# Condition row first, first group of x in four loads, weight table in 2 KB runs (conditioned residual, one core)

## What is computed

```python
W = weights[condition]                       # (64, 128, 128)
x = x + jnp.einsum('bct,bcd->bdt', x, W)     # (64, 128, 2048)
```

## Time and profile before

| | us |
|---|---|
| median of three runs | 320.84 |
| the profiled execution, its own time | 320.35 |
| its span, first to last instruction | 318.6 |
| PE busy in the span | 244.4 |
| VectorE busy | 146.8 |
| GpSimd busy | 19.0 |

### The profile page before, as it was taken

The page is one execution under the profiler, slowest core; times in us unless marked ns, Lnnn a source line. Parts: engine busy times, 40 slices in busy tenths (PEclk is TensorE's granted clock), DMA queues, the critical chain, the costliest instruction groups (busy, mean ns, idle before and its releaser), DMA issues.

```text
span 318.6 us, 1351 instructions
## 1 busy us (share of the span) xinstructions
PE 244.4 (77%) x512; PEld 103.8 (33%) x512; DVE 146.8 (46%) x65; POOL 19.0 (6%) x69
## 2 busy tenths in 40 slices
PE   0059999996884979969399795948979597596980
PEld 0024444442432424324143342413424242242430
DVE  0005676676261462637326373550745547055371
POOL 0000000000000000000001000000000000001000
PEclk9999999999997897999869799995989999699897
DMA  8999999999999999999999999999999999999997
GB/s 313 436 436 440 416 395 444 411 426 420 440 424 436 444 416 448 424 432 436 428 448 416 444 424 436 444 416 453 416 440 428 432 448 411 453 420 436 440 403 313
DMA packets 5187, 135.29 MB, mean 425 GB/s; under 512 B 578, under 2 KB 578, under 8 KB 578
## 3 DMA queue, kind: packets, MB, share of 16 engines
q10 hardware_dynamic: 2882, 68.16, 49.7%
q1 hardware_dynamic: 2304, 67.11, 49.4%
HBM read 68.16 MB, written 67.11 MB: 425 GB/s over the span
## 4 chain that ended last, share of the span: by engine, by line
DMA 61%; PE 33%; DVE 3%; POOLq 0%; issue 0%; ACTq 0%; POOL 0%
PE product L90 33%; DMA out<-x_ring 29%; DMA x_ring<-x 27%; DMA condition_row<-condition 5%; DVE x_ring L106 3%; POOLq L72 0%; ACTq L111 0%; POOL chosen_weights L78 0%; DVE state_row L100 0%; POOLq L71 0%; POOLq L78 0%; POOLq L77 0%
## 5 line engine op out<-in xcount | busy, mean ns | idle before, releaser
L90 PE MATMUL product<-x_ring,chosen_weights 128*128 128x512 f32 x512 | 244.4, 640 | 64.9 <-DMA x_ring<-x 45.3
L106 DVE TENSOR_TENSOR x_ring<-product,x_ring 128x2048 f32<-128x2048 f32 x64 | 146.7, 2292 | 147.4 <-PE product L90 147.4
L90 PEld LDWEIGHTS product<-x_ring,chosen_weights 128*128 128x128 f32 x512 | 103.8, 205 | 204.6 <-issue 141.1
L78 POOL COPY chosen_weights<-weight_table 128x128 f32 x64 | 18.8, 294 | 286.0 <-DVE x_ring L106 267.2
L100 DVE TENSOR_SCALAR state_row<-condition_row 1x64 int32<-1x64 int32 x1 | 0.2, 182 | 17.3 <-DMA condition_row<-condition 17.3
L137 POOL MEMSET const-float32-0.0<- 128x1 f32 x1 | 0.1, 98 | 0.1
L137 POOL MEMSET const-bfloat16-1.0<- 128x1 bf16 x1 | 0.1, 101 | 0.0
L137 POOL MEMSET const-uint8-127<- 128x1 uint8 x1 | 0.1, 101 | 0.0
L137 POOL MEMSET const-float32-1.0<- 128x1 f32 x1 | 0.1, 98 | 0.0
L137 POOL BASE_LOAD x1 | 0.0, 12 | 0.1
## 6 DMA issues: line engine op xcount, KB each, us to landing
x_ring<-x SPq DMA_DIRECT2D x16, 4096.0 KB, 28.2
out<-x_ring ACTq DMA_DIRECT2D x15, 4096.0 KB, 29.8
out<-x_ring ACTq DMA_DIRECT2D x4, 1024.0 KB, 7.9
weight_table<-weights ACTq DMA_DIRECT2D x1, 1024.0 KB, 15.1
condition_row<-condition ACTq DMA_DIRECT2D x1, 0.2 KB
```

Source lines behind the costliest of these rows:

```text
L78: pool.tensor_copy(chosen_weights[b][:, :], weight_table[:, bass.ds(state[b] * features, features)]).then_inc(weights_chosen[b], 1)
L90: last = pe.matmul(product[:, b % psum_slots, m * BANK_COLUMNS:(m + 1) * BANK_COLUMNS], chosen_weights[b][:, :], x_ring[:, bass.ds(b * tim ...
L106: dve.tensor_tensor(tile, product[:, b % psum_slots, :], tile, AluOpType.add).then_inc(sum_done[b], 1)
```

## The change

1. ACT issues the condition's load first, then the weight table's.
2. Group 0 of `x` is loaded with four DMAs of 1 MB, one for each batch (8 KB for each channel), in place of one of 4 MB. The first increments `x_loaded[0]`; the other three have a new semaphore each (`head_loaded`), on which PE waits before batches 1 to 3 of every turn (satisfied for good after the first).
3. The launch lays the weight table out in 4 parts of 4 states each: part, channel, state within the part, feature. The table's DMA takes for each channel four runs of 2 KB (512 runs) in place of one of 8 KB (128 runs). Its place in SBUF and its bytes are the same.

```diff
+TABLE_PART = 4
...
-    _, states, features = weights.shape
+    parts, _, part_states, features = weights.shape
+    states = parts * part_states
...
+        head_loaded = [sem(f"head_loaded{i}") for i in range(1, GROUP)]
...
-            for g in range(groups):
+
+            for i in range(GROUP):
+                sp.dma_start(x_ring[:, i * time:(i + 1) * time], x[0, :, i * time:(i + 1) * time]
+                             ).then_inc(head_loaded[i - 1] if i else x_loaded[0], 16)
+            for g in range(1, groups):
...
                     if b % GROUP == 0:
                         pe.wait_ge(x_loaded[b // GROUP], 16 * (turn + 1))
+                    elif b < GROUP:
+                        pe.wait_ge(head_loaded[b - 1], 16)
...
-            act.dma_start(weight_table[:, :], weights.rearrange("c s d -> c (s d)")
-                          ).then_inc(table_loaded, 16)
             act.dma_start(condition_row[0:1, :], condition.rearrange("(o b) -> o b", o=1)
                           ).then_inc(condition_loaded, 16)
+            act.dma_start(weight_table[:, :].rearrange("c (p k) -> c p k", p=parts),
+                          weights.rearrange("p c s d -> c p (s d)")
+                          ).then_inc(table_loaded, 16)
...
+    table = np.asarray(L0_cond_weights)
+    states, _, features = table.shape
+    table = table.reshape(states // TABLE_PART, TABLE_PART, channels, features).transpose(0, 2, 1, 3)
...
-        "weights": np.ascontiguousarray(np.asarray(L0_cond_weights).transpose(1, 0, 2)),
+        "weights": np.ascontiguousarray(table),
```

## The result

The changed kernel takes 324.48 us (median of four runs, 324.35 to 324.91) against 320.83 us for the kernel before. The ratio is 1.0114, interval 1.0091 to 1.0138. The forecast was 320.3 us in a range of 319.0 to 322.0, with "the same" as the likeliest case and 0.12 on "slower". The time lies 2.5 us outside the range, on the side that I held least likely. (Of the later kernels, the one profiled execution of e12 was a disturbed one, 326.64 us against 320.39 to 322.29 for its others, so only the first 40 us of its trace are read.)

A forecast was written before the change was run, and what follows sets the result against it. The prediction took the transfer of 135.29 MB at 433 GB/s as the bound. Span 318.6 - 0.86 (dip) + 0.14 + 0.14 (short runs) = 318.0, plus 1.75 outside and 0.49 to the median: 320.3 us, range 319.0 to 322.0.

The forecast's parts named there:

- The bound and the floor: Whole kernel: transfer of 135.29 MB at 433 GB/s is the bound; with every dip gone the floor is 319.0 us.
- Turns run by run: Table's load beside x at the start: the two queues alternate run by run, not byte by byte.
- My landing time: Start: the table lands at 14.5 to 15.5 us, so the first matmul comes near 17.2, some 2.5 us earlier.
- The condition first: nothing at the end: Start, ACT's queue: the table's load starts about 0.5 us later, SP's loads fill that time; cost at the end nothing.
- The dip of 38 to 44 us regained: Low stretch near group 0's store: a store issued at about 35.7 us regains 0.86 us.
- Both queues stay filled: Middle, loop of four rooms: load 4 is queued 8.5 us before landing near 77.5; the rate stays 433 GB/s.
- nothing happens early: Rival, start: table lands as late as 17.3 us, first matmul near 19.7, no dip goes; 321.1 us, chance 0.03.
- A gap for each added DMA: Rival, group 0's loads: three more handovers leave engines dry, 2.6 us plus 0.28 for runs; 323.7 us, chance 0.06.
- The dear 2 KB runs: Rival, table's load: a 2 KB run costs what 8 KB does, partly or wholly; up to 328.2 us, chance 0.03.
- Three more DMAs on SP's queue: Group 0's loads: each next DMA is queued before the one before ends; 384 more short runs cost 0.14 us.
- One bound of the range: Upper bound 322.0 us: 2 KB runs costing a seventh of the way up to 8 KB, no handover regained.

The follow-up runs named there:

- e12: The changed kernel with the condition's load issued behind the table's again on ACT's queue: 321.69 us, ratio 1.0023.
- e10: The changed kernel with the table's load at the head of SP's queue, ahead of x, and in 8 KB runs: 320.22 us, ratio 0.9985.
- e11: The changed kernel with the table in 8 KB runs and the condition's load behind the table's again: 320.09 us, ratio 0.9984.
- e2: The changed kernel with the table in 8 KB runs again, nothing else altered: 322.09 us, ratio 1.0039.
- e7: The kernel before with the table's load moved to the head of SP's queue, ahead of x, in 8 KB runs: 320.20 us, ratio 0.9986.
- e9: The changed kernel with the table's load, still in 2 KB runs, moved to the head of SP's queue: 320.42 us, ratio 0.9998.
- e5: The kernel before with GpSimd making two copies of the table ahead of its loop, delaying the first matmul: 322.81 us, ratio 1.0056.
- e4: The changed kernel with group 1 of x in four loads of 1 MB too: 321.57 us, ratio 1.0022.
- e8: The kernel before with the table's load at the head of SP's queue, in 512 runs of 2 KB: 320.47 us, ratio 0.9997.
- e1: The kernel before with only the condition's load put ahead of the table's on ACT's queue: 321.63 us, ratio 1.0027.
- e3: The changed kernel with group 0 of x in one load of 4 MB again: 346.09 us, ratio 1.0776.
- e6: The kernel before with GpSimd making four copies of the table ahead of its loop, delaying the first matmul: 323.57 us, ratio 1.0100.

## Why the prediction was wrong

- **The bound and the floor: right, but for 44 to 62 us,** where PE's pace set the time. The middle ran at 433 GB/s in both kernels, and the sum over the stretches closed to 0.3 us. The first matmul 11.4 us earlier (e10) brought 0.3 us, and the floor of 319.0 was not crossed by any median.
- **Turns run by run: right,** and the most useful reading of the trace (231 against 230 packets). The kernel before has it too: from 5 to 8 us the 16 engines moved on average two runs each of x and two of the table.

```profile
q1 hardware_dynamic: 32, 1.05, 80.9%
q10 hardware_dynamic: 32, 0.26, 20.6%
```

  My landing time failed on the count, and this is the first step that failed. I wrote "each engine has 32 runs of the table against the 32 of group 0 ... from about 2 us on". Both queues would have had to start together. x had a lead of 8.3 runs for each engine, and all of these 8.3 turns were then paid at the estimated 1.29 us. The error is 8.3 x (1.29 - 0.39) = 7.5 us, plus 3 us for turns that began at 5 us and not at 2: 14.5 us becomes 25.0, and 24.5 was measured.
- **The lead was in my own rows.** I let the table's turns begin at about 2 us, while in the next paragraph I took 4 us from a store's issue to its first packets for the dip at 38 to 44 us. The trace of the kernel before had it for the table too: issued at 0.78 us, it has no packet before 3 us, when x had 16.
- **"The condition first: nothing at the end": wrong.** I counted 0.5 us of issue. The first packets of the table came 2 us later (e12 against the changed kernel) to 3 us later (e11 against e2), and in the changed kernel each microsecond of x's lead was multiplied, since a turn against 8 KB is 0.39 us and a turn against 32 KB is 1.29, both by the estimate from the earlier trace rows.
- **The dip of 38 to 44 us regained: the number was luck** (0.92 against 0.86). I had it filled by an earlier store. But the store came 6.7 us later, and only loads filled the stretch. Nor does an early store fill it: e7 issued its first store at 34.56 us, ahead of my 35.7, and from 38 to 44 us it still ran at

```profile
38.00:44.00 6.00, 6.00 (x15) 2.66 (x14) 3.75 (x2) 0.59 (x2) 1.00 0.93 388
```

  The kernels with group 0 in four loads have 426 to 437 GB/s there, wherever their first store stands (27.18 to 44.94 us); those with one load have 366 to 415. What is won there is missing before: 4 to 38 us ran at 427 in place of 437 GB/s, 0.79 us where I had 0.28 for short runs, and over 4 to 44 us together the two kernels are at 427 and 429. Even e9 to e11 are no more than 0.16% faster.
- **"Both queues stay filled": wrong. This is the second step that failed, and it made the first error cost time:** 3.5 of the 4.2 us are lost from 44 to 62 us. I checked it for a first store at 35.7 us, that is for my own forecast of the table, and didn't ask from which start on it fails. The rival "nothing happens early" put the table at 17.3 us and stopped there. The edge lay less than 2.6 us beyond the store of the kernel before (e5). A rival "the table lands later than now" would have had a clear mechanism and, at 44.94 us, a price near the 3.7 us measured.
- **The rivals.** A gap for each added DMA (323.7) had nearly the measured time but not the cause: e4 has four DMAs more and is faster. The dear 2 KB runs cost 0.27 us (e8 against e7), 328.2 was far off.
- **Three more DMAs on SP's queue: no cost shows.** e9 against e8 has three DMAs more and takes 320.42 us against 320.47.
- **One bound of the range** is 0.2 us too low for what it is said to take in: a seventh of the way for the 2 KB runs (1.0 us) and no handover regained (0.86) give 322.2 and not 322.0. It decides nothing here.

What stays open: why a load of 256 bytes ahead of the table's moves its first packets by microseconds; why the kernels e1, e4 and e12, with a first store at 38.2 to 39.3 us, lie 1 us above the kernel before at 38.24, and how much of that is the edge that e5 found; and how e2 loses its 2 us. One hint at the edge: the kernel before itself reaches 322.44 us in single executions, while e7 to e11, with first stores at 27 to 35 us, reach no more than 321.5. But e2, with its store at 31.43 us, doesn't fit this.

## What to carry to other kernels

In these traces two DMA queues that compete took turns by contiguous run (231 against 230 packets in the changed kernel, 144 against 144 in e3), and a transfer's share was its run length against the other's: the same megabyte landed 43.7 us after its issue in 2 KB runs beside 32 KB ones (e3), 9.4 us in 8 KB runs beside 8 KB ones (e2), and 4.7 us at the head of x's own queue (e7). So a small table that others wait for goes ahead of the bulk in the same queue, or in long runs, and not in shorter ones beside a bulk load. Issue it as the first thing of its queue, since here even a load of 256 bytes ahead of it moved its first packets by 2 to 3 us. This kernel, bound by transfers, hid an early start (a first matmul 11.4 us earlier in e10 brought 0.3 us) and showed a late one once nothing was queued (a first store at 43.83 us in place of 38.24 cost 3.1 us in e6, against the executions beside it): ask how much later the first store may come before the queues run dry, and price that side too.

## What the runs showed of the hardware

- 1 MB lands after 4.7, 7.6, 9.4, 15.1, 23.1 or 43.7 us from its issue (e7, e11, e2, before, changed, e3). Its own bytes are the same each time; what differs is its queue, what is issued ahead of it, and the run lengths on both sides.
- 2 KB runs alone in the queue: 0.8 us more for 512 of them than for 128 of 8 KB.
- The last writes don't come together. In e7, small writes to semaphores (the last columns count packets under a size) come as 14 from 315.4 to 315.9 us, and the last two from 316.9 to 317.9:

```profile
DMA packets 26, 0.10 MB, mean 197 GB/s; under 512 B 14, under 2 KB 14, under 8 KB 14
...
DMA packets 4, 0.02 MB, mean 16 GB/s; under 512 B 2, under 2 KB 2, under 8 KB 2
```

  If the last store's 16 small writes are one for each engine, fourteen engines were done 1 to 2.5 us before the last. This unevenness may be what remains of the room between 320.1 us and the floor; no run here tested it.
